# A graph network's first part, done once per launch, in another order

## The reference

```
x = norm(x + adj @ (x @ W0) + b0)                     # layer 0
x = norm(x + L1(x[:25], adj[:25,:25]) on 25 nodes)    # layer 1: 5 node groups of 25, 9, 7, 6 and 6 nodes,
    # per group: symmetric normalisation of adj_g + I by row sums, two graph convolutions 128->256->128, ReLU,
    # summed with softmax weights
x = norm(x + attention(x, adj))                       # layer 2: weights adj * exp(e_i + f_j), rows normalised
x = norm(x + L3(x))                                   # layer 3: two convolutions along the nodes (17 taps),
                                                      # messages between neighbours by distance, a gated update
```

## Time and profile before

| what | us |
|---|---|
| median of 3 timed runs (range) | 648.75 (646.16 to 649.4) |
| the profiled execution, its own time | 646.53 |
| its span, first to last instruction | 644.7 |
| first block, until the loop's first matmul | 103.28 |
| mean granted TensorE clock | 0.961 |

### The profile page before, as it was taken

The page is one execution under the profiler, slowest core; times in us unless marked ns, Lnnn a source line. Parts: engine busy times, 40 slices in busy tenths (PEclk is TensorE's granted clock), DMA queues, the critical chain, the costliest instruction groups (busy, mean ns, idle before and its releaser), DMA issues.

```text
span 644.7 us, 11585 instructions
## 1 busy us (share of the span) xinstructions
PE 605.6 (94%) x3553; PEld 494.5 (77%) x3553; DVE 491.4 (76%) x1833; ACT 314.0 (49%) x635; POOL 111.8 (17%) x118
## 2 busy tenths in 40 slices
PE   3799798999999999999999999999999999999893
PEld 2689686878797879797878787878787887879672
DVE  4547653878888888878888889797979797978753
ACT  2201363464646465556464645555464646464331
POOL 2410101121121212030212120212121212112100
PEclk9757898999999999999999999999999999999998
DMA  7880002200303030303030303030201102000000
GB/s 193 244 262 2 1 1 89 91 1 1 100 2 98 0 98 0 98 0 98 0 98 0 98 0 98 0 96 2 70 28 40 58 22 78 6 13 1 18 17 16
DMA packets 33522, 34.50 MB, mean 54 GB/s; under 512 B 1882, under 2 KB 22753, under 8 KB 33368
## 3 DMA queue, kind: packets, MB, share of 16 engines
q1 hardware_dynamic: 33154, 34.03, 17.1%
q10 hardware_dynamic: 342, 0.15, 0.1%
HBM read 29.79 MB, written 4.39 MB: 53 GB/s over the span
## 4 chain that ended last, share of the span: by engine, by line
PE 44%; issue 22%; DVE 11%; POOL 3%; ACT 3%; DVEq 0%; POOLq 0%; ACTq 0%
PE bank L247 6%; PE bank L249 5%; PE bank L248 5%; PE pair L247 4%; PE pair L249 4%; PE pair L248 4%; PE bank L1582 4%; POOL rs L1085 3%; PE pair L1518 3%; DVE x L1236 2%; DVE st L1219 2%; PE bank L1453 2%; PE bank L1485 2%; PE bank L1523 1%; DVE mv L1225 1%
## 5 line engine op out<-in xcount | busy, mean ns | idle before, releaser
L1085 POOL TENSOR_TENSOR rs<-ve,neg_half 128x4 f32<-128x4 f32 (+1 forms) x61 | 58.1, 952 | 332.4 <-DVE ve L1231 299.6
L247 PE MATMUL bank<-cd_hi,w_hi 128*128 128x256 f32 x272 | 81.3, 299 | 0.0
L249 PE MATMUL bank<-cd_hi,w_lo 128*128 128x256 f32 x272 | 76.8, 282 | 0.0
L248 PE MATMUL bank<-cd_lo,w_hi 128*128 128x256 f32 x272 | 76.7, 282 | 0.0
L247 PEld LDWEIGHTS bank<-cd_hi,w_hi 128*128 128x128 f32 x272 | 51.6, 190 | 11.8 <-issue 11.7
L1582 PE MATMUL bank<-P,msg 128*128 128x512 f32 x128 | 57.6, 593 | 0.2 <-issue 0.2
L247 PE MATMUL pair<-aT_hi,x_hi 128*128 128x512 f32 x128 | 52.3, 409 | 0.0
L248 PE MATMUL pair<-aT_lo,x_hi 128*128 128x512 f32 x128 | 51.6, 403 | 0.0
L248 PEld LDWEIGHTS bank<-cd_lo,w_hi 128*128 128x128 f32 x272 | 51.5, 189 | 0.0
L249 PE MATMUL pair<-aT_hi,x_lo 128*128 128x512 f32 x128 | 51.5, 402 | 0.0
L249 PEld LDWEIGHTS bank<-cd_hi,w_lo 128*128 128x128 f32 x272 | 51.3, 189 | 0.0
(11 more groups left out here) (326 smaller groups left out, 1543.0 us busy)
## 6 DMA issues: line engine op xcount, KB each, us to landing
adj_nat<-in_adj_dram SPq DMA_DIRECT2D x16, 1024.0 KB, 5.8
x_nat<-in_x_dram SPq DMA_DIRECT2D x16, 256.0 KB, 3.0
out_dram<-y_out SPq DMA_DIRECT2D x16, 256.0 KB, 2.4
xt<-in_x_dram SPq DMA_DIRECT2D x3, 1280.0 KB, 10.3
hw<-in_L_gnn_W_dram SPq DMA_DIRECT2D x2, 640.0 KB, 14.2
xt<-in_L_gnn_conv_w_dram SPq DMA_DIRECT2D x1, 1088.0 KB, 6.9
aT<-in_adj_dram SPq DMA_DIRECT2D x5, 150.0 KB
nat_ih<-in_L_gnn_w_ih_dram SPq DMA_DIRECT2D x1, 384.0 KB, 5.2
```

The source lines that it names most:

```text
L247: nc.tensor.matmul(o, lh, rh, start=start, stop=False)
L248: nc.tensor.matmul(o, lh, rl, start=False, stop=False)
L249: return nc.tensor.matmul(o, ll, rh, start=False, stop=stop)
L1085: g.tensor_tensor(rs[i][:, 0:n], ve[i][:, 0:n], neg_half[:, 0:n], ALU.pow).then_inc(po_rs[i], 1)
```

## The change

Only the first block changes, and in it the order, the source of the 25x25 blocks, the width of the own sums and who adds the tap sums. In short:

1. The six small DMAs into `A0` are gone. The blocks are taken from the loaded strips `adjP`, whose first 25 columns are broadcast over five places and masked by a block-diagonal mask `BD` folded into `GM`.
2. `own_sums` multiplies 100 moving columns in place of 25 (the wanted 25 are picked out by `copy_sums`, now two copies).
3. TensorE does graph 0's `three` before it waits for the strips.
4. Graph 0's hidden layer writes bank 2 and no longer waits for the copied own sums; it goes ahead of the `v12` product.
5. `block_rows(1..3)`, `scale_columns`, own sums 1 and 2 move behind graph 0's layer 1. All own sums and outputs stand ahead of `pe_agg2`, and the own rows' norm on VectorE ahead of graph 0's `y3`.
6. Weight groups 2 and 3, `transpose_second(2)` and `(3)`, the 17-tap scaling and `x_lo` of graph 1 move into the loop over the five groups; the tap sums (`nat_sum`) go from VectorE to GpSimd.

```diff
-        LATE = [[4], [5], [6, 7], [8], []]
+        LATE = [[], [2, 3], [4, 5], [6, 7], [8]]
+        LATE_AT = [[2], [3], [], [], []]
 # SyncE
-                sp.wait_ge(q_zero, 1)
-                sp.dma_start(A0[0:NODES, 0, 0:NODES], ...)
-                for j in range(PJ):
-                    sp.dma_start(A0[NODES * j:NODES * (j + 1), 1:NT, NODES * j:NODES * (j + 1)], ...)
 # GpSimd
+                g.affine_select(out=BD3, in_=BD3, compare_op=ALU.is_ge, fill=0.0, base=0,
+                                pattern=[[-NODES, PJ], [0, NODES]], channel_multiplier=1).then_inc(q_bd, 1)
+                ...   # a second one with the other bound
+                g.tensor_tensor(nat_sum, nat_c2[:, :, 0:TAPS - 1:2], nat_c2[:, :, 1:TAPS:2], ALU.add)
 # ScalarE
-                    s.activation(TTs[:, t, :], TT_BANK[t][:, 0:R], ACT.Identity).then_inc(q_TTs, 1)
+                    s.activation(TTs[:, t, 0:R - NODES]..., TT_BANK[t][:, 0:(PJ - 1) * R]...[:, :, 0:NODES], ACT.Identity)
+                    s.activation(TTs[:, t, R - NODES:R], ...).then_inc(q_TTs, 1)
+                act.wait_ge(pe_agg1, 1)
+                s.activation(agg_sb[:, :], AG_BANK[:, :], ACT.Identity).then_inc(ac_agg1, 1)
                 copy_rows(0)
                 copy_rows(1)
                 ...
+                copy_sums(1)
+                round_weights(-1)
+                copy_sums(2)
                 act.wait_ge(dv_f, 1)
                 s.activation(pef[:, 1, :], ef[:, 1, :], ACT.Exp, bias=c12[:, 1:2]).then_inc(ac_pf, 1)
 # VectorE
+                def mask_blocks(t):
+                    for gi in range(NG):
+                        last = v.tensor_tensor_reduce(A5[0:R, t, gi, :]..., bc(AB[0:R, t, :], PJ), GM[0:R, gi, :]..., 1.0, 0.0,
+                                                      ALU.mult, ALU.add, deg[0:R, 3, NG * t + gi:NG * t + gi + 1])
+                v.tensor_tensor(GM[0:R, :, :], GM[0:R, :, :], bc(BD[0:R], NG), ALU.mult).then_inc(q_gm, 1)
-                v.tensor_tensor(A0[0:R], A0[0:R], bc(ident[0:R, 0:R], NT), ALU.add).then_inc(q_A1, 1)
+                v.tensor_tensor(AB[0:R, 1:NT, :], adjP[0:R, :, 0:NODES], bc(EY[0:R], PT), ALU.add).then_inc(q_A1, 1)
+                mask_blocks(1)         # mask_blocks(2) behind nadjT of graph 0, mask_blocks(3) behind x2
 ...
                 veP, scale_columns(2), scale_columns(3), nadjT group 4, rest_of_weights(0), x1P, dot(0, c), then dq and y3
 # TensorE, own sums
-                            last = t_.matmul(TT_BANK[t][:, NODES * j:NODES * (j + 1)], xt[t][:, j, mc, :],
-                                             aPT[t % 2][:, mc, NODES * j:NODES * (j + 1)], ...)
+                            lo = 0 if j < PJ - 1 else NODES
+                            last = t_.matmul(TT_BANK[t][:, 100 * j:100 * (j + 1)], xt[t][:, j, mc, :],
+                                             aPT[t % 2][:, mc, lo:lo + 100], ...)
 # TensorE, order after the change, by the names of the helpers and lines before
+                transposes L902, three x4 (agg1), transpose_rows(0), (1), L921, block_rows(0), own_sums(0, (0,)), L917,
+                own_sums(0, (1,)), transpose_rows(2), own_sums(0, (2, 3)), L928, own_sums(0, (4,)), L942, L935/L936, L952,
+                own_sums(1, (0,)), L958, block_rows(1), (2), (3), own_sums(1, 1..4), own_sums(2, all), transpose_weights(-1),
+                own_outputs, transpose_weights(0), three x4 (agg2), transpose_second(0), L979, transpose_weights(1),
+                L1003/L1004, hidden(0), transpose_second(1), then the five groups
```

More of the change, by code:

```diff
@@ L634, in _ @@
                                 spread(deg[0:NODES, 3, 0:NG], NODES), ALU.mult).then_inc(q_nT, 1)
-                dve.wait_ge(q_colsb, 1)
-                dve.nop(nofuse=True)
-                for j in range(2):
-                    last = v.tensor_scalar(abc[:, j, :], ones[:, :], cols[:, A1 + j:A1 + j + 1], None, ALU.mult)
-                last.then_inc(q_abc, 1)
+                mask_blocks(2)
                 hold(dve, po_rs[0], 1)
@@ L646, in _ @@
                 last.then_inc(dv_x1r, 1)
+                mask_blocks(3).then_inc(q_A5, 1)
+                degrees(R, NG, NT * NG, 2)
+                dve.wait_ge(q_colsb, 1)
+                dve.nop(nofuse=True)
                 v.tensor_scalar(bn_bias[:, :], cols[:, V1:V2 + 1:V2 - V1], EPS, None, ALU.add).then_inc(q_bnv, 1)
-                inverse_degrees(R, NG, NT * NG, 2)
-                for t in range(1, NT):
-                    v.tensor_tensor(A5[0:R, t], A5[0:R, t], spread(deg[0:R, 3, NG * t:NG * (t + 1)], R), ALU.mult).then_inc(q_B, 1)
+                for j in range(2):
+                    last = v.tensor_scalar(abc[:, j, :], ones[:, :], cols[:, A1 + j:A1 + j + 1], None, ALU.mult)
+                last.then_inc(q_abc, 1)
                 dve.wait_ge(q_cst2, 16 * 3)
@@ L696, in _ @@
                 last.then_inc(q_own, 1)
+                scale_columns(1)
                 dve.wait_ge(q_own, 5)
@@ L761, in _ @@
                 v.tensor_scalar(veP[0:R, :], mvP[0:R, :, 1], EPS, None, ALU.add).then_inc(q_nP, 1)
+                scale_columns(2)
+                scale_columns(3)
+                v.tensor_tensor(nadjT[0:R, 1:NT, 4, :], bank[3][0:R, 0:PT * R].rearrange("p (a b) -> p a b", a=PT),
+                                spread(deg[0:R, 3, NG + 4:NT * NG:NG], R), ALU.mult).then_inc(q_nT, 1)
+                rest_of_weights(0)
+                hold(dve, q_rsP, 1)
+                for t in range(PT):
+                    last = v.tensor_scalar(x1P[0:R, t, :], x1P[0:R, t, :], mvP[0:R, t, 0:1], rsP[0:R, t:t + 1], ALU.subtract,
+                                           ALU.mult)
+                last.then_inc(q_nP, 1)
+                for c in range(NC):
+                    last = dot(0, c)
+                last.then_inc(dv_e, 1)
                 hold(dve, pe_out2, 1)
@@ L929, in _ @@
                           start=True, stop=True).then_inc(q_U0, 1)
-                own_sums(0, (3, 4))
+                own_sums(0, (4,))
+                pe.wait_ge(q_U0s, 1)
+                pe.wait_ge(q_h1, 16)
+                pe.wait_ge(ac_aT[2], 1)
+                for i in range(2 * NG):
+                    last = t_.matmul(bank[2][:, NODES * i:NODES * (i + 1)], hw1[:, i // 2, ch(i % 2)], U0[:, i // 2, :],
+                                     start=True, stop=True)
+                last.then_inc(q_hid0, 1)
                 pe.wait_ge(q_abc, 1)
@@ L937, in _ @@
                 last.then_inc(q_v, 1)
-                pe.wait_ge(q_U0s, 1)
-                pe.wait_ge(q_h, 16 * 2)
-                pe.wait_ge(q_TTs, 1)
-                for i in range(2 * NG):
-                    last = t_.matmul(bank[4][:, NODES * i:NODES * (i + 1)], hw1[:, i // 2, ch(i % 2)], U0[:, i // 2, :],
-                                     start=True, stop=True)
-                last.then_inc(q_hid0, 1)
-                block_rows(1)
-                block_rows(2)
+                pe.wait_ge(q_h2, 16)
                 pe.wait_ge(q_own, 3)
@@ L959, in _ @@
                 last.then_inc(q_o0, 1)
-                pe.wait_ge(q_c12, 1)
-                own_sums(1, range(PJ))
+                block_rows(1)
+                block_rows(2)
+                block_rows(3)
+                own_sums(1, range(1, PJ))
+                pe.wait_ge(q_nT, 2)
+                own_sums(2, range(PJ))
                 pe.wait_ge(q_own, 5)
@@ L964, in _ @@
                 transpose_weights(-1)
-                pe.wait_ge(q_nT, 2)
-                own_sums(2, (0, 1, 2))
+                pe.wait_ge(q_TTs, 2)
+                for t in range(PT):
+                    last = own_outputs(t)
+                last.then_inc(q_o, 1)
+                pe.wait_ge(q_whi, 1)
+                pe.wait_ge(q_wt, 16 * 3)
+                pe.wait_ge(q_sc1, 2)
+                transpose_weights(0)
                 pe.wait_ge(dv_pf, 1)
@@ L1013, in _ @@
                         hidden(gi + 1)
+                    for mc in LATE_AT[gi]:
+                        transpose_second(mc)
                     for k in LATE[gi]:
```

266 lines of the change are left out of this document (128 added, 138 removed).

## The result

The changed kernel took 623.27 us (median of 4 runs, 622.53 to 629.23) against 648.12 us (4 runs, 646.16 to 649.4): a ratio of 0.9639, 95% interval 0.9575 to 0.9704. Its profiled execution took 623.29 us, span 621.3, mean granted clock 0.990; that of before 646.53, 644.7 and 0.961. (A ratio is always to the kernel before, timed in the same session.) In a later session the same kernel gave 623.61 us (6 runs, ratio 0.9637, 0.9600 to 0.9673).

The account below looks back on a forecast made before the run. TensorE bounds the first block, through half clock and waits by order. Chained steps end the block at 79.7 against 102.0 us, 22.3 saved, taken as 22: 648.75 - 22 = 626.75, say 627 us; range 623.5 to 638.5.

Parts of the forecast that it names:

- Graph 0's sum first: Early first block: TensorE's sum for graph 0, run before the strips, ends at 18.3 us against 25.5, 7.2 us earlier.
- Strips: Strip loads early in the block: landing at 19.3 us as upper bound; from 18.3 down TensorE doesn't wait for them.
- Own sums: TensorE's own sums with 100 columns: 0.115 us per instruction taken, bounds from no added cost to 0.11 to 0.13 us.
- The clock: TensorE's clock in the first block: full from about 18 us to its end; clock kept, chance 0.55, 625 to 630 us.
- Rival 1: Clock falls in TensorE's waits for VectorE's scaling, 35.8 to 38.7 us; block ends at 87, time 634 us; chance 0.20.
- rival 2: Wider columns don't hold the clock, which falls behind each tile's own sums; block ends at 91.7, 638.5 us; chance 0.10.
- The new wait: Before the second aggregation: ScalarE's exponential, behind the last own sums' copy, starts at 48.4 us, not 45.5; 2.9 us.
- Own rows' norm first: After the second aggregation: addition at 50.5 us against 69.66, first matmul on the norm at 56.2 against 77.69.
- Groups: Block's last stretch, five groups: starts at 61.5 us against 85.13, chain 1.7 us longer, VectorE last at 79.7.
- Loads: DMA loads of the first block: graph 1's adjacency, wanted at 52.5 us, isn't late, with only 5 us of cover.
- Rival 4: A load in the first block comes 4 to 8 us late, giving 631 to 635 us; chance 0.09.
- The transposes: By a skill rule they don't count as clock activity, so the clock would be lost at 18 to 25 us and in the groups.

## Why the prediction was right, point by point

- *Graph 0's sum first.* Right in kind, 1.8 us too late in size: it ended at 16.5, forecast 18.3. It began at 12.74 in place of 13.4, and the pitch of the twelve instructions went from 0.43 to 0.23 us at 14.4, where I had let the clock rise at 17.5. The 1.8 us bought nothing: TensorE then waited 2.00 us for the strips.
- *Strips.* 18.49, inside the bounds of 18.3 and 19.3, with a price of the six dropped loads possible but not shown.
- *Own sums.* 0.114 us with 100 columns against the 0.115 taken. The bound of 0.13 is refuted.
- *The clock.* Forecast full from 18 us to the block's end; it was, but for 31.5 to 34.9 and the last 0.7 us. L959 took 2.33 us (forecast 2.3, before 4.44). L975 took 3.94 where I had 2.2: the one step that failed. It cost nothing, since VectorE was then busy with the fusion weights and the scaling; its L720 began at 38.62, forecast 38.8, before 51.02. Rival 1 was this mechanism at large: the clock falls in the waits between 35.8 and 38.7, and the own sums behind them stay at half clock. No fall came there; the clock was back at 34.9, ahead of them, so whether these 72 own sums would have lifted it wasn't put to the test. One argument against this rival was misread: the 6.7 us from 48.1 hold no wait of TensorE to speak of, as it is busy for 6.60 of them. With 25 or 50 columns the clock was lost behind or in the own sums; rival 2 is the result of those kernels (block 91.7 forecast, 88.28 and 90.53 measured).
- *The new wait.* VectorE waited 3.63 us for the exponential (forecast: at 48.4 and 2.9 us later than it could; it ran at 47.91). Its price at the end is 0.65 us by the kernel that fills it and 1.2 by the one that removes it, counted from the end of the own sums; the medians show neither.
- *Own rows' norm first.* x1P's addition at 49.97 (50.5), L1023 at 55.08 (56.2), L891 at 60.47 (61.5): 0.5, 1.1 and 1.0 us early. The strips and `xt[0]` were each 0.8 us earlier than I took them, but that isn't the reason: the 72 own sums ran from 38.83 to 47.01, forecast 38.7 to 47.0. The time came off behind them: the exponential 0.5 us earlier, and 5.1 us in place of 5.7 from x1P's addition to L1023. Undoing it costs 9.8 us, the most of the moves undone singly.
- *Groups.* VectorE was the last, as forecast, at 78.74 (79.7); 17.28 of its 19 us are busy. From L891 to there it took 18.3 us, forecast 18.2. The 1.7 us "longer than before" in the forecast is against the chained old order (101.6); against the row read (102.04), which the sum uses, it is 1.3, and 1.4 were measured. The added VectorE work was put at some 8.5 us; in this stretch it came to 5.9 (16.8 us busy against 11.0).
- *Loads.* TensorE, VectorE and ScalarE waited for no DMA behind 22 us. GpSimd waited for `xP` until 36.77 (38.40 before). Rival 4 didn't come.
- *The transposes.* Of the 144 instructions of the groups' stretch 36 are transposes on the identity, and the clock was 1.00 throughout. The rule of the Trainium skill ("TensorE: Matmul & The Clock Gate", section Part 4) that they don't count as activity had no cost here (the kernel before had 28 in its stretch from 82.3 to 102.7, not only the 20 of the weights); that they count isn't shown either, as products stand between them.

**The size.** The block's saving was 23.3 us, forecast 22.3 and rounded down to 22; the legs up to the last own sum were right to 0.2 us from 38.8 on, and those behind it 0.5 to 1.1 us too late. That is 1.3 of the 3.5 us by which 626.75 missed. The other 2.2 come from the base: I subtracted from the median of 648.75, while the profile on which the legs rest is an execution of 646.53, and the kernel after has its profiled run at its median. So the median of 623.27 is 0.2 us under the range's low end of 623.5. The term at fault is the base, not a mechanism.

## What to carry to other kernels

A busy TensorE isn't one that keeps its clock. Where many small products follow each other and each costs the same with more moving columns, read the clock behind them; streaming columns that are thrown away (75 of 100 here) was worth 8.3 to 10.4 us of a block of some 100, at no cost in the products themselves. An idle stretch of several us can be paid twice, once as the wait and once as half clock behind it (6.0 us late at its end here, and 3.7 more behind it), so order the queue by what has landed, and put first what most of the later matmuls hang on. Before work is moved to GpSimd or earlier, look at what VectorE will then do beside it: twice here about half of the gain went that way. And take a saving off the execution it was read from, not off another median.

## What the runs showed of the hardware that I had not expected

- A product of this kind (128-row weights) took 0.114 to 0.115 us with 25, 50 and 100 moving columns at clock 1.00, and 0.20 (25 columns) or 0.23 (50) at 0.50. What differed was the clock afterwards, and 50 columns were no better than 25.
- In the ten profiles with graph 0's sum first, the clock stayed at 1.00 behind waits for the strips of 2.00, 2.04, 2.05, 2.26 and 2.42 us, and fell to 0.50 between 0.8 us ahead of the strips' first transpose and 0.9 us behind it with waits of 2.96, 3.38, 3.63, 4.46 and 4.73. The work around them differs; no run varied the wait alone.
- The printed clock is 1.00 from the start, though TensorE runs at half pace until its first rise, seen only in the pitch (0.43 to 0.23 us at 14.4 us).
- GpSimd's first root (25x5) took 4.16 us in the kernel before and 4.15 in the one with width alone, where VectorE ran 15 masks of the earlier trace rows in a row beside it; it ended 1.0 us behind the last of them. In the eleven profiles of the new order, where VectorE does little then, it took 1.16. So it looks as if GpSimd had stood back until the masks were through; that the two share something is inferred from the times. Not every mask does it: in the kernel after, the root at 23.22 us (128x4) takes 1.02 us with five masks of the new form, which read one operand as a broadcast, beside it; in the kernel before, without masks, it takes 1.05 and 1.01. It also goes the other way: 1.09 us against 0.28 for VectorE's 128x128 dot (at 36.91, beside GpSimd's addition of `xP`), 1.23 against 0.56 and 2.62 against 1.11 above.

```profile
16.82 4.16 POOL L387 TENSOR_TENSOR deg<-deg,neg_half 25x5 f32<-25x5 f32 x1 [7.35 <-DVE deg L538]
```

```profile
15.82 1.16 POOL L392 TENSOR_TENSOR deg<-deg,neg_half 25x5 f32<-25x5 f32 x1 [6.86 <-DVE deg L548]
```

The two rows are from GpSimd's timelines of the kernel before and of the kernel after. Those 3 us cost the old order nothing: VectorE wanted the root only for graph 0's own scaling, and TensorE stood in its wait for the strips until 19.36.
